# Groups of four token tiles in place of two for GpSimd's inverse spreads and scatters, in a fused graph-attention and mixture-of-experts kernel

## The reference

```
x = x + graph_attention_0(layernorm(x))          # masked softmax over the 128 nodes of a graph, elu
x = x + mixture_0(layernorm(x))                  # top 2 of 8 experts per row, 128 -> 256 -> 128, gelu
x = x + graph_attention_1(layernorm(x))          # as the first, relu
x = x + mixture_1(layernorm(x))                  # top 1 of 32 experts per row, 128 -> 32 -> 128, relu
```

## Time and profile before

| | |
|---|---|
| median of 3 runs | 1195.77 us |
| lowest and highest | 1187.94 and 1197.13 us |
| span of the profiled execution | 1195.3 us, mean granted PE clock 0.837 |
| first output write of mixture 0 on DVE (L951), last | 345.0 us, 641.2 us |
| first scatter (L506), last | 354.0 us, 650.2 us |
| first load of the third stage (L311) | 652.4 us |

### The profile page before, as it was taken

One profiled execution on the slowest core, in us unless ns is written; L12 is line 12 of the kernel. 1 busy time (PEld: TensorE's weight loads), 2 busy tenths in 40 slices (PEclk: granted clock), 3 DMA queues, 4 the chain that ended last, 5 costly groups with the idle time before them and its releaser, 6 DMA issues. The chain is left out here.

```text
span 1195.3 us, 27365 instructions
## 1 busy us (share of the span) xinstructions
PE 948.1 (79%) x6789; PEld 839.2 (70%) x6789; DVE 791.0 (66%) x3492; ACT 708.2 (59%) x2414; POOL 781.6 (65%) x989
## 2 busy tenths in 40 slices
PE   5888988887179999999994899999960667666873
PEld 4677877776079999999994688888850555544653
DVE  6688898889459999999994378888873121121221
ACT  3998898886035656555552899999930333322431
POOL 4357777777617787877776048778785366666666
PEclk9999897987579999999997999999975655666555
DMA  9133432211367777777772113232213442223210
GB/s 207 37 120 118 139 102 61 60 51 38 95 180 207 203 205 206 208 203 207 196 203 60 36 51 87 76 86 76 60 42 109 109 111 83 74 82 85 64 35 8
DMA packets 147913, 130.88 MB, mean 109 GB/s; under 512 B 26450, under 2 KB 119484, under 8 KB 147760
## 3 DMA queue, kind: packets, MB, share of 16 engines
q1 hardware_dynamic: 125456, 93.02, 30.4%
q0 software_dynamic: 18272, 34.21, 8.4%
q10 hardware_dynamic: 4032, 1.89, 0.5%
HBM read 83.28 MB, written 49.61 MB: 111 GB/s over the span
## 5 line engine op out<-in xcount | busy, mean ns | idle before, releaser
L477 POOL DMA_INDIRECT xs<-staged,dst x256 | 258.9, 1011 | 77.6 <-issue 68.5
L1067 ACT ACTIVATE hT<-bank,wt 128x128 f32<-128x128 f32 x620 | 177.2, 369 | 133.4 <-PE bank L1274 81.4
L528 POOL DMA_INDIRECT out<-oq,xq x160 | 159.9, 999 | 112.2 <-DVE oq L978 66.3
L506 POOL DMA_INDIRECT x2d<-ob,xi x155 | 163.6, 1055 | 43.3 <-issue 29.1
L1260 PE MATMUL bank<-xnT,wt 128*128 128x128 f32 x1240 | 166.9, 278 | 0.7 <-issue 0.4
L1274 PE MATMUL bank<-w2s,hT 128*128 x1240 | 165.5, 276 | 0.7 <-DVE ob L951 0.5
L978 DVE SCALAR_TENSOR_TENSOR oq<-bank,xq 128x512 f32<-128x512 f32 x40 | 27.7, 692 | 197.1 <-remote 103.2
L1260 PEld LDWEIGHTS bank<-xnT,wt 128*128 128x128 f32 x1240 | 152.6, 194 | 3.1 <-issue 2.5
L1274 PEld LDWEIGHTS bank<-w2s,hT 128*128 128x128 f32 x1240 | 150.9, 192 | 1.8 <-issue 1.2
L1101 ACT ACTIVATE xnqT<-bank 128x512 f32<-128x512 f32 x40 | 23.9, 596 | 164.0 <-remote 71.0
L1016 ACT ACTIVATE p<-bank,nm 128x128 f32<-128x128 f32 x256 | 103.1, 403 | 19.1 <-DVE nm L699 13.9
(11 more groups left out here) (202 smaller groups left out, 2313.9 us busy)
## 6 DMA issues: line engine op xcount, KB each, us to landing
wt<-wpd SPq DMA_DIRECT2D x155, 258.0 KB
xq<-xs SPq DMA_DIRECT2D x160, 66.0 KB
xi<-xs SPq DMA_DIRECT2D x155, 66.0 KB
xb<-x2d SPq DMA_DIRECT2D x32, 258.0 KB
xb<-in_x SPq DMA_DIRECT2D x32, 256.0 KB
wpd<-w1c SPq DMA_DIRECT2D x56, 129.0 KB
xs<-staged,dst POOLq DMA_INDIRECT x256
out<-oq,xq POOLq DMA_INDIRECT x160
```

Source lines behind the costliest of these rows:

```text
L477: pool.indirect_dma_start(out=xs[l], out_offset=bass.IndirectOffsetOnAxis(ap=dst[b % ND][:, c:c + 1], axis=0), in_=stag[s][:, q, 0:ROW], i ...
L506: pool.indirect_dma_start(out=x2d, out_offset=bass.IndirectOffsetOnAxis(ap=xi[t % NXI][:, ID:ID + 1].bitcast(U32), axis=0), in_=ob[:, t % ...
L528: pool.indirect_dma_start(out=orow, out_offset=bass.IndirectOffsetOnAxis(ap=xq[j % NXQ][:, q, ID:ID + 1].bitcast(U32), axis=0), in_=oq[j % ...
L1067: last = act.activation(hT[t % 2][:, j, :], HID[t % 2][:, j, :], ACT.Gelu, bias=wt[t % NW][:, c:c + 1])
```

## The change

POOL takes the tiles in groups of four (`FOURS`: 38 groups of four, then one of two, tiles 152 and 153, and one of one, tile 154). For each group it adds eps to all variances at once, raises them at once, and then scatters all tiles of that same group, one after the other. No scatter stands between the two small operations any more. `mv2` and `ve2` are four wide for it. `ob` has 16 buffers in place of 14, so that a group of four is contiguous. The eight landing semaphores count by group, and the end waits for the last eight groups.

```diff
--- before.py
+++ after.py
@@ -46,8 +46,8 @@
 
 XW = P + 1
 
-TWOS = [(t, 2) for t in range(0, NTILE[0] - 1, 2)] + [(t, 1) for t in range(NTILE[0] // 2 * 2, NTILE[0])]
-OF_TILE = [(j, t - a) for j, (a, k) in enumerate(TWOS) for t in range(a, a + k)]
+FOURS = [(t, 4) for t in range(0, 152, 4)] + [(152, 2), (154, 1)]
+OF_TILE = [(j, t - a) for j, (a, k) in enumerate(FOURS) for t in range(a, a + k)]
 
 NX, NS, ND = 7, 10, 4
 
@@ -244,7 +244,7 @@
             v1raw = raw("v1raw", [P, E1 * H1])
 
 
-        NXI, NW, NO = 20, 6, 14
+        NXI, NW, NO = 20, 6, 16
         with ExitStack() as first_mixture:
 
             def fm(name, shape):
@@ -259,8 +259,8 @@
             ya = [fm(f"ya{s}", [P, P]) for s in range(2)]
             ob = fm("ob", [P, NO, XW])
             st2 = [fm(f"st2_{s}", [P, 6]) for s in range(2)]
-            mv2 = [fm(f"mv2_{s}", [P, 2, 2]) for s in range(2)]
-            ve2 = fm("ve2", [P, 2])
+            mv2 = [fm(f"mv2_{s}", [P, 4, 2]) for s in range(2)]
+            ve2 = fm("ve2", [P, 4])
         TX = [bank[0][:, 0:P], bank[1][:, 0:P]]
         HID = [bank[2][:, :].rearrange("p (j s) -> p j s", j=4), bank[3][:, :].rearrange("p (j s) -> p j s", j=4)]
         YB = [bank[4][:, 0:2 * P], bank[5][:, 0:2 * P]]
@@ -289,7 +289,7 @@
         def rows_out(t):
 
             j = OF_TILE[t][0]
-            return sem(f"x2_out{j % 8}"), 16 * sum(TWOS[a][1] for a in range(j % 8, j + 1, 8))
+            return sem(f"x2_out{j % 8}"), 16 * sum(FOURS[a][1] for a in range(j % 8, j + 1, 8))
 
 
         vflat = vt[:, :, :].rearrange("p e c -> p (e c)")
@@ -376,8 +376,8 @@
                 sp.dma_start(xi[t % NXI][:, :], xs0[bass.ds(row[t % 8], P), :]).then_inc(sem(f"tile_in{t % NXI}"), 16)
                 after(sp, "gelu", t - NW)
                 sp.dma_start(wt[t % NW][:, :], wpd[bass.ds(wrow[t % 8], P), :]).then_inc(sem(f"wt_in{t % NW}"), 16)
-            for t in range(NTILE[0] - 15, NTILE[0], 2):
-                sp.wait_ge(*rows_out(t))
+            for a, k in FOURS[-8:]:
+                sp.wait_ge(*rows_out(a))
 
 
             for n in range(NG, 2 * NG):
@@ -498,29 +498,23 @@
 
             graph_layer(0)
 
-            def rows_leave(j, half):
-
-                a, k = TWOS[j]
+            def rows_leave(j):
+
+                a, k = FOURS[j]
                 after(pool, "x2_rstd", j)
-                for t in range(a + half, min(a + half + 1, a + k)):
+                for t in range(a, a + k):
                     pool.indirect_dma_start(out=x2d, out_offset=bass.IndirectOffsetOnAxis(ap=xi[t % NXI][:, ID:ID + 1].bitcast(U32), axis=0),
                                             in_=ob[:, t % NO, :], in_offset=None, bounds_check=NTOK - 1,
                                             oob_is_err=False).then_inc(sem(f"x2_out{j % 8}"), 16)
 
 
-            for j in range(len(TWOS) + 1):
-                if j < len(TWOS):
-                    a, k = TWOS[j]
-                    after(pool, "ob", a + k - 1)
-                    after(pool, "x2_rstd", j - 1)
-                    pool.tensor_tensor(ve2[:, 0:k], mv2[j % 2][:, 0:k, 1], eps[:, 0, 0:k], ALU.add).then_inc(sem("x2_ve"), 1)
-                if j > 0:
-                    rows_leave(j - 1, 0)
-                if j < len(TWOS):
-                    after(pool, "x2_ve", j)
-                    pool.tensor_tensor(ob[:, a % NO:a % NO + k, P], ve2[:, 0:k], neghalf[:, 0:k], ALU.pow).then_inc(sem("x2_rstd"), 1)
-                if j > 0:
-                    rows_leave(j - 1, 1)
+            for j, (a, k) in enumerate(FOURS):
+                after(pool, "ob", a + k - 1)
+                after(pool, "x2_rstd", j - 1)
+                pool.tensor_tensor(ve2[:, 0:k], mv2[j % 2][:, 0:k, 1], eps[:, 0, 0:k], ALU.add).then_inc(sem("x2_ve"), 1)
+                after(pool, "x2_ve", j)
+                pool.tensor_tensor(ob[:, a % NO:a % NO + k, P], ve2[:, 0:k], neghalf[:, 0:k], ALU.pow).then_inc(sem("x2_rstd"), 1)
+                rows_leave(j)
             graph_layer(1)
             for j in range(QUADS):
                 after(pool, "oq", j)
```

## The result

The changed kernel takes 1283.55 us (median of 4 runs, 1275.67 to 1286.21) against 1196.12 us (4 runs, 1187.94 to 1197.13, the three of the table above and one more) on the same chip: ratio 1.072, 95% interval 1.069 to 1.076. The forecast was 1196.2. The profiled execution is the one of 1275.67 us, its span 1273.9 us, 78.6 us more than before.

A forecast was written before the change was run, and what follows sets the result against it. PE was taken to bound the steady stretch at 1.933 us a tile, POOL the tail. Nothing from the stretch plus 0.44 us from the tail, on 1195.77 us, gave 1196.2 us; range 1187 to 1201.

The forecast's parts named there:

- 6.40 us stand against 4 x 1.933 = 7.73 us of PE's: First mixture's steady stretch: POOL's group of four takes less time than PE's four tiles, so the change gives nothing.
- Bursts of scatters land late: Rival, first mixture: late landings of four scatters in a row stop SP's loads; 38 us more, 1234 us; chance 0.02.
- Behind a power a scatter starts after 0.19 us: POOL in the first mixture: pause of 0.19 us between a power and the next scatter, counted in the group's 6.40 us.
- The tail term: After the first mixture's last tile: POOL's last scatter starts at 650.59 in place of 650.15, 0.44 us later.
- the bound of 1.8: Upper bound of the tail's loss in us, with a power of 1.27 us and all seven scatters at 1.16.
- The power of four: POOL's power of four columns in the first mixture: 1.05 to 1.27 us, costed at 1.05.
- Neither SP nor DVE waits for a landing: Expected sign in the first mixture: buffers freed later still come in time, some 5 us left for SP's queue.
- The longer power blocks DVE: Rival, steady stretch: DVE's `xn` waits during powers, 0.52 us for each of 38 groups, 20 us, 1216 us; chance 0.06.
- PE's floor of 1.90 us: PE's shortest time per tile in the first mixture; reaching it everywhere would gain 5 us, 1191.2 us; chance 0.10.

The follow-up runs named there:

- e11: The kernel before with a bounds check added to the graph stages' scatters: 1141.27 us, against 1137.41 us for the kernel before on that chip.
- e8: The changed kernel with plain POOL stores to consecutive rows in place of the indirect scatters: 1185.67 us, against 1195.81 us for the kernel before.
- e10: The changed kernel with the scatters' row numbers from a table and no bounds check: 1142.55 us, against 1137.41 us for the kernel before.
- e14: The changed kernel without adds and powers, each scatter following its own tile's aggregate: 1191.65 us, against 1201.19 us for the kernel before.
- e13: e10 unaltered, on a chip where the kernel before takes 1196.22 us: 1272.17 us (2 runs), ratio 1.063 to the kernel before.
- e9: The changed kernel with the scatters' row numbers from a table, bounds check kept: 1145.05 us, against 1137.41 us for the kernel before.

## Why the prediction was wrong, step by step

**"6.40 us stand against 4 x 1.933 = 7.73 us of PE's. POOL gets freer (1.3 us in every four tiles) and remains behind PE, so this gives nothing."** This is the step that failed: the term put at nothing is 0.532 us a tile, some 82 us in the profiled execution, nearly all of the loss (78.6 us between the two spans, 87 us between the medians). POOL does remain behind PE. Its group takes some 7.1 us and not 6.40 (the group shown above adds at 430.65 and ends its last scatter at 437.76), still under 7.73, and it then waits for DVE's aggregate 2.9 us a group (57.5 us in 20, above). But a scatter was costed as POOL's time and a landing alone. What the change really did was to move most scatters from 1.44 to 2.11 us apart (5th and 75th percentile, 400 to 600 us) to 1.28 to 1.40, and in this loop that has a price on PE's consumers that no busy time contains.

**"Bursts of scatters land late."** The rival looked at the right edit for the wrong wait. Nothing landed too late: SP waits only for ACT's gelu in the kernel after too (103.0 us in all, no wait longer than 3.6). I dismissed it with "scatters start no closer than 1.27 us apart, hardly nearer than today's". The 5th and 25th percentile of today's spacing in the mixture are 1.44 and 1.79 us; the 1.27 is a pause of 0.30 and a duration of 0.97 added up. A rival that is judged by spacing must have the spacings of this loop beside it.

**The trace of before held a warning** in a part that the change doesn't touch. I had its rows before me and didn't follow them up. In the second mixture POOL issues scatters 1.29 us apart. Timeline of the kernel before:

```profile
1001.25 1.91 PE L1304 MATMUL bank<-xnqT,vq 128*32 128x128 f32 x8
...
1002.78 0.98 POOL L528 DMA_INDIRECT out<-oq,xq  x1 [0.30 <-issue]
...
1004.07 0.98 POOL L528 DMA_INDIRECT out<-oq,xq  x1 [0.30 <-issue]
1004.14 1.03 PEld L1294 LDWEIGHTS bank<-vt,hqT 33*128 33x128 f32 x8 [0.33 <-issue]
1004.14 1.23 PE L1294 MATMUL bank<-vt,hqT 33*128 x8
1005.36 0.98 POOL L528 DMA_INDIRECT out<-oq,xq  x1 [0.30 <-issue]
1006.65 0.98 POOL L528 DMA_INDIRECT out<-oq,xq  x1 [0.30 <-issue]
```

PE is done at 1005.37 and nothing of DVE or ACT starts before 1010.56, while scatter follows scatter. ACT's copy `xnqT` (L1101), which starts then, waits for nothing but results of PE by the code. Waits of the kernel before, 950 us to the end:

```profile
DVE oq L978 <- remote: 103.2, 15, 8.8
ACT xnqT L1101 <- remote: 71.0, 10, 9.2
```

This kernel runs on one core, so "remote" names nobody: the wait ended with no instruction to show for it, and I had not asked why. (DVE's wait at L978 can by the code also be for a landing.) In e11 on the chip without the effect, whose last stage is the same, the waits have no such line; the largest is

```profile
ACT xnqT L1102 <- PE bank L1154: 95.8, 39, 11.6
```

and the last stage takes 226 us in place of 265.

**"Behind a power a scatter starts after 0.19 us."** Wrong row. In the kernel before the scatter behind a power belongs to the pair ahead of it and doesn't wait for that power, whatever releaser the row names. With the true wait it is 0.79 us. POOL's timeline at the end of the kernel after:

```profile
717.94 0.20 POOL L514 TENSOR_TENSOR ve<-mv,eps 128x4 f32<-128x4 f32 x1 [2.18 <-DVE mv L956]
718.21 1.24 POOL L516 TENSOR_TENSOR ob<-ve,neghalf 128x4 f32<-128x4 f32 x1
720.24 1.04 POOL L506 DMA_INDIRECT x2d<-ob,xi  x1 [0.79 <-POOL ob L516]
...
725.14 0.22 POOL L514 TENSOR_TENSOR ve<-mv,eps 128x2 f32<-128x2 f32 x1
...
730.95 1.04 POOL L506 DMA_INDIRECT x2d<-ob,xi  x1 [0.79 <-POOL ob L516]
```

The group takes 7.20 us where 6.40 was forecast, and from add to last scatter 13.01 us where 11.02 was forecast and 10.58 was measured before. The tail term is +2.4 us, not +0.44: three first scatters that come 0.60 later than costed make 1.8 of the 2.0 that were missing, the power of 1.24 in place of 1.05 the rest. It is also outside the bound of 1.8 that I gave.

**What held.** The power of four takes 1.05 us on average (36 of them, 1046 ns). Neither SP nor DVE waits for a landing. "The longer power blocks DVE" didn't happen, but the changed kernel was no test of it: `xn` averages 255 ns (L902 above), and from 345 to 690 us not one of its 139 `xn` lies beside a power. What speaks against the rival is in the kernel before, where nine `xn` begin within a power of two columns and take 0.25 to 0.27 us, no longer than those that meet nothing of POOL's; all 50 `xn` of over 0.35 us there began during a scatter. The rule of the Trainium skill, "SBUF — State Buffer", section "Who interferes with whom", by which a power would block such an `xn`, is not borne out by these nine. The landing and the load behind the last scatter are 2.21 and 2.78 us (2.08 and 2.80 in the earlier trace rows). PE's floor of 1.90 us is real: e8 and e10 run at it, and so does e11, whose first mixture is that of the kernel before.

**What stays open.** The cause is shown as far as the kernel goes: in this loop, on the chips that have the effect, it is the closeness of the indirect scatters. What in the chip holds back PE's results isn't shown. The records of PE end on time and those of its consumers begin late; whether it is the semaphore update, its delivery, or the last write to PSUM can't be read from them. Nor is it known where between 1.57 and 1.9 us the hold ends, why one chip lacks it, and why the graph stages, whose scatters are as close, are spared; on that chip (e11) the first stage is 7 us shorter and the third 4 us. No run of these was a version of the whole function that beats the kernel before: its order, one scatter between the small operations and one behind them, is the one that spaces them.

## What to carry to other kernels

Cost an indirect scatter of POOL's not by its own microsecond but by the distance to its neighbours as well: before putting scatters in a row, list their spacings in the loop and see what waits for PE meanwhile. That is a reason to try it, not a rule: the graph stages of this same kernel bear scatters as close without harm. Waits of DVE and ACT that name PE long after PE's record has ended, or that name nothing ("remote"), are to be explained before an edit of POOL's order is called free. And take the price of a wait from a row in which that very wait exists, not from one that merely has the same two operations behind one another.

## What the runs showed of the hardware

- In the first mixture, in series of indirect scatters of 128 rows from POOL, 1.26 to 1.57 us apart, the engines that wait for PE start late, up to some 3 us at a time (the copy's longest wait 2.8 us, the gelu's 3.8, in the change). Mostly 1.6 to 2.1 us apart (e14 and the kernel before) nearly nothing is lost. Four plain stores from POOL 0.55 us apart do no harm (e8). In the graph stages scatters as close delay nothing by more than 0.10 us at L1005.
- The effect depends on the chip. On the chip of the result and on four of those of the experiments the kernel before takes 1195.8 to 1202.2 us, and on one of them a burst variant takes 1272 (e13). On the chip of e9 to e11 it takes 1137.41 and the same variant 1142.55 (single runs). Of these 59 us 39 are in the last stage, by the trace of e11; the change leaves that stage alone.
- A scatter with a bounds check starts 0.79 us behind a power that it waits for (the change, e9), one without it 0.29 (e13).
